# A transformer block on one core: four engines taken off their fixed slot and given one written-out order for all eight batches

## The reference

```python
# branch 1: one-head attention and a layer norm
att = softmax((xn Wq)(xn Wk)^T / sqrt(128))
y   = einsum('bqk,bvd->bqd', att, v)        # k and v summed apart: row sums of att times the sum of v
h   = xn + y Wfc^T + b_fc
o1  = layernorm(h) * gamma + beta
# branch 2: causal attention with 16 heads of 8, then four experts
hn  = rms(xn) * n1_w
q, k, v = rms(heads(hn wq)) * qn_w, rms(heads(hn wk)) * kn_w, heads(hn wv)
ao  = softmax(where(causal, q k^T / sqrt(8), -inf)) v wo^T ; ao[:, :, :32] = 0
x1  = xn + ao ; xf = rms(x1) * n2_w
wts = top 2 of softmax(xf gate^T), scaled to sum 1
moe = sum_e wts[e] * expert_e(xf)           # gelu, silu and two chains of gelu layers
moe[:, :, :32] = 0
out = x + o1 + x1 + moe
```

## Time and profile before

| what | value |
|---|---|
| median of 3 runs | 232.24 us (230.71, 232.24 and 232.61) |
| span of the profiled execution, first to last instruction | 231.3 us |
| PE busy | 202.3 us, 87% of the span |
| DVE busy | 160.1 us, 69% |
| ACT busy | 160.1 us, 69% |
| POOL busy | 112.9 us, 49% |
| mean granted TensorE clock | 0.991 |

### The profile page before, as it was taken

The page is one execution under the profiler, slowest core; times in us unless marked ns, Lnnn a source line. Parts: engine busy times, 40 slices in busy tenths (PEclk is TensorE's granted clock), DMA queues, the critical chain, the costliest instruction groups (busy, mean ns, idle before and its releaser), DMA issues.

```text
span 231.3 us, 6236 instructions
## 1 busy us (share of the span) xinstructions
PE 202.3 (87%) x2132; PEld 145.6 (63%) x2132; DVE 160.1 (69%) x608; ACT 160.1 (69%) x310; POOL 112.9 (49%) x227
## 2 busy tenths in 40 slices
PE   0542898859999999999999999999999999997883
PEld 0311455436867787678767776867686777766563
DVE  2245059795858897789868995899489667847704
ACT  2123447745989698978898789878987998732730
POOL 3834225872572747282837282737375437506000
PEclk9999999997999999999999999999999999999999
DMA  4900100000000020002000200020000000100000
GB/s 124 389 16 11 37 3 1 4 0 0 4 0 3 3 68 6 0 3 68 0 3 6 68 4 0 3 68 4 0 3 27 23 4 0 48 0 3 23 0 27
DMA packets 7570, 6.09 MB, mean 26 GB/s; under 512 B 624, under 2 KB 7024, under 8 KB 7536
## 3 DMA queue, kind: packets, MB, share of 16 engines
q1 hardware_dynamic: 7248, 5.44, 7.5%
q10 hardware_dynamic: 288, 0.21, 0.3%
HBM read 4.60 MB, written 1.05 MB: 24 GB/s over the span
## 4 chain that ended last, share of the span: by engine, by line
PE 73%; DVE 11%; issue 5%; ACT 4%; POOL 3%; DMA 2%; SPq 0%; POOLq 0%; ACTq 0%; DVEq 0%
PE even_ps L1357 12%; PE scores_ps L1242 10%; PE pv_ps L1271 7%; PE odd_ps L1343 7%; PE a_ps L1212 6%; PE even_ps L1343 5%; PE even_ps L1387 4%; PE odd_ps L1387 3%; PE odd_ps L1369 3%; PE a_ps L1184 3%; PE pv_ps L1275 3%; PE a_ps L1286 3%; DMA first<-in_first 2%; DVE acc L1054 2%; PE a_ps L1202 2%
## 5 line engine op out<-in xcount | busy, mean ns | idle before, releaser
L325 POOL TENSOR_SCALAR_AFFINE_SELECT probs<-probs 128x512 f32<-128x512 f32 x64 | 40.3, 635 | 47.4 <-ACT probs L507 46.7
L507 ACT ACTIVATE probs<-scores_ps 128x768 f32<-128x768 f32 x64 | 49.9, 809 | 5.1 <-PE scores_ps L1242 4.9
L1242 PE MATMUL scores_ps<-qT,kT 32*128 32x128 f32 (+1 forms) x512 | 31.4, 361 | 0.3 <-ACT probs L507 0.2
L1357 PE MATMUL even_ps<-l_h,mid 128*128 128x256 f32 x128 | 30.7, 383 | 1.0 <-ACT l_h L569 1.0
L1242 PEld LDWEIGHTS scores_ps<-qT,kT 32*128 32x128 f32 x512 | 24.2, 192 | 10.4 <-issue 9.1
L1357 PEld LDWEIGHTS even_ps<-l_h,mid 128*128 128x128 f32 x128 | 23.4, 190 | 6.2 <-ACT l_h L569 2.1
L1343 PE MATMUL odd_ps<-xfT,up 128*128 128x256 f32 x80 | 22.1, 391 | 0.4 <-DVE acc L1054 0.4
L1271 PE MATMUL pv_ps<-probs,v_aug 128*32 128x256 f32 x256 | 21.3, 406 | 0.9 <-DVE pv_rows L834 0.4
L569 ACT ACTIVATE l_h<-even_ps 128x512 f32<-128x512 f32 x24 | 14.5, 606 | 8.1 <-PE even_ps L1357 7.1
L1212 PE MATMUL a_ps<-qkvT,xnT 128*128 128x384 f32 x32 | 17.5, 635 | 2.1 <-ACT qkv L543 1.5
L1343 PE MATMUL even_ps<-xfT,up 128*128 128x256 f32 x64 | 18.8, 418 | 0.0
(11 more groups left out here) (150 smaller groups left out, 451.4 us busy)
## 6 DMA issues: line engine op xcount, KB each, us to landing
x_sb<-in_x SPq DMA_DIRECT2D x8, 128.0 KB, 2.5
acc<-in_x SPq DMA_DIRECT2D x8, 128.0 KB, 2.1
out<-acc SPq DMA_DIRECT2D x8, 128.0 KB, 1.9
mid<-in_mid SPq DMA_DIRECT2D x1, 640.0 KB, 7.5
up<-in_up SPq DMA_DIRECT2D x1, 578.0 KB, 6.4
downs<-in_down SPq DMA_DIRECT2D x1, 512.0 KB, 8.3
first<-in_first SPq DMA_DIRECT2D x1, 320.0 KB, 5.5
row<-in_rows ACTq DMA_DIRECT2D x1, 200.0 KB, 5.2
```

What stands on the lines that cost most here:

```text
L325: nc.gpsimd.affine_select(out=own, in_=own, compare_op=ALU.is_ge, fill=0.0, base=0, pattern=[[0, 2 * TILES], [1, P]], channel_multiplier=- ...
L507: nc.scalar.activation(probs[g % 2][:, 2 * half:2 * half + 2, 0:SEQ + P], scores_ps[:, 2 * half:2 * half + 2, 0:SEQ + P], ACT.Exp).then_in ...
L1242: ins = T.matmul(ps, kT[p][rows, g, kt * P:(kt + 1) * P], qT[p][rows, kt * P:SEQ], start=kt == 0, stop=kt == 1 and not searching, tile_pos ...
L1357: ins = T.matmul(ps_of(fill)[:, m * SEQ:(m + 1) * SEQ], wT[:, at_col:at_col + P], src[:, ci, :], start=(ci == 0), stop=(ci == HC - 1))
```

## The change

All four engines lose `slot` and get one list of steps for the eight batches, written out call by call (`batches()` on PE and DVE, plain lines on POOL and ACT). The lists have no period: which stage of which batch stands beside which differs from batch to batch. With it:

- The bank of a fill is fixed by name, and its turn is counted as PE's list is issued (`claim`). Bank a holds QKV0, QKV1, QKT, PV0 and PV1, bank b eight narrow fills, even and odd as before.
- `weigh_v` writes two groups into one bank, and `pv_turn` turns 512 columns at once, twice a batch and not four times. `exp_group` takes 1536 columns in one ACTIVATE, `mask` one group in one instruction.
- `probs` has four copies, x_sb, xn and acc eight (so x is loaded once, not twice, and all loads are issued at the start), xnT four, qkv, v_aug, qT, kT, q0T and xfT three, most others two.
- The head normalisation has one cubic and one Newton round, seven steps after the guess, and no halving step. The gate loses two steps (the inverse of the sum and its product) and does four comparisons in two instructions. `fc_row` broadcasts the row sum as its stationary operand, so `a0_xsum` is gone. `scores` of a group waits for that group's copy of k alone.
- In the head DVE clears v_aug (three copies) and computes the flag from a small DMA of its own; PE and DVE read the flag before their first step of `batches()`, and the branch without a search comes first. POOL builds all constants before its first norm step.

```diff
-BANK_FILLS = {
-    "a": (("QKV1", 1), ("Q0T", 1), ("S00", 2), ("S01", 2), ("FC", 2), ("QKT", 1), ("XT", 0), ("QKV0", 0)),
-    "pv": (("PV0", 2), ("XFT", 3), ("GATE", 3), ("PV1", 2), ("PV2", 2), ("PV3", 2), ("WO", 2)),
...
+BANK_OF = {
+    "QKV0": "a", "QKV1": "a", "QKT": "a", "PV0": "a", "PV1": "a",
+    "XT": "b", "Q0T": "b", "S00": "b", "S01": "b", "FC": "b", "XFT": "b", "GATE": "b", "WO": "b",
...
             def weigh_v(n, g):
...
+                pair, half = divmod(g, 2)
+                fill = f"PV{pair}"
+                ps = (claim(fill, n) if half == 0 else ps_of(fill))[:, half * SEQ:(half + 1) * SEQ]
+                pe.wait_ge(s["masked"], GROUPS * n + g + 1)
...
-                ins.then_inc(full_sem(fill), 1)
+                if half == 1:
+                    ins.then_inc(full_sem(fill), 1)
...
+            def batches():
+                x_turn(0); qkv_project(0, 0); fold_weights(); q0_project(0); qkv_project(0, 1); a0_scores(0, 0)
+                a0_scores(0, 1); x_turn(1); qk_turn(0); q0_project(1); find_maxima(0); scores(0, 0); x_turn(2)
...
-            def exp_unit(n, u):
...
+            def mask(n, g):
+
+                pool.wait_ge(s["exp_done"], GROUPS * n + g + 1)
...
+            constants()
+            search_constants(); ln_variance(0); ln_pow(0); h_square(0); h_mean(0); h_eps(0); x1_start(0); h_pow(0)
...
+            def exp_group(n, g):
+                act.wait_ge(s["scores_full"], GROUPS * n + g + 1)
+                if n >= 1:
+                    act.wait_ge(full_sem(f"PV{g // 2}"), at[f"PV{g // 2}", n - 1] + 1)
+                nc.scalar.activation(probs[g][:, :, 0:SEQ + P], scores_ps[:, :, 0:SEQ + P], ACT.Exp
+                                     ).then_inc(s["exp_done"], 1)
...
+            def clear_heads(p):
+
+                V.memset(v_aug[p][:], 0.0).then_inc(s["dve_setup"], 1)
...
+            def pv_turn(n, pair):
```

1945 lines of the change are left out of this document (896 added, 1049 removed), and 4 rows, old and new, of tables (BANK_FILLS, BANK_OF).

## The result

The change takes 233.63 us (median of 20 executions) against 232.69 for the kernel before: ratio 1.0068, 95% interval 1.004 to 1.0096. It is 0.7% **slower**; 228.0 was forecast. The profiled execution has a span of 231.5 us, 0.2 above the 231.3 of before.

The account below looks back on a forecast made before the run. It took PE's work, some 190 us, as the bound, with gains only at the two ends: 231.3 - 5.1 (head) + 2.5 (middle) - 1.6 (tail) = 227.1 of span, plus 0.9 to the median, 228.0 us; range 219 to 236.

Parts of the forecast that it names:

- the middle: Between head and tail: ten more ACT table loads, mostly hidden, cost PE 2.5 us of waits; DVE and POOL at nothing.
- the tail: Batch 7's last layers: held-back down pairs of batch 6 fill gaps, one wait of about 2 stays; 1.6 us won.
- the head: Start to xf(0): 2.1 us sooner, plus 3.0 of PE work done ahead, gives 5.1 us.
- The start: Constants and first norm: first transpose near 7.35, 1.0 us sooner; DVE's branch taken as 0, up to 4.1 possible.
- The loop of scores: Batch 0's scores and exponentials: first scores at 23.9, rounds about 3.5, last scores 34.5, last values 38.0, 2.1 us sooner.
- The chain from there to xf ... unchanged: From batch 0's last values to xf(0): same steps, still 10.9 us, so xf(0) is turned at 48.9.
- the bank of E1A: In the tail, a kernel bank, not a run: L2 of batch 7 waits about 2 us until DVE frees it.
- From span to median: At the sum: 0.9 us added to the span of 227.1, giving a time of 228.0.
- second rival: Head's gain given back: batch 1's chain to xf stays 10.9, PE waits 4 us; span 231, time 232; chance 0.21.
- first rival: ACT's table loads end on PE's path: 239 us, deciding from 9.1 us of PE waits in the middle; chance 0.17.
- 250: Time in us if each extra table load also cost the skill page's drain; chance 0.01.

Follow-up runs that it names:

- e2: The changed kernel with tanh in place of gelu in all experts, so 37 of its 38 table loads go; ratio to the kernel before 0.998, span 230.2 us.
- e3: The kernel before the change with tanh in place of gelu, so 27 of its 28 table loads go; ratio 0.993.
- e9: The changed kernel with DVE's steps for batch 7's heads moved ahead of nine steps of batch 6's gate; 231.11 us, ratio to the kernel before 0.994.
- e13: e9 with 9 unread matmuls added in PE's pauses at 13.7 to 18.9 us; 229.70 us, ratio to the kernel before 0.988.
- e15: e13 with 8 more unread matmuls (4, 1 and 3) in PE's pauses between 30 and 38.7 us; 229.20 us, ratio to the kernel before 0.989.

## Why the prediction was wrong

The span was to be 227.1 and is 231.5. Of these 4.4 us the middle has 2.3 (4.8 lost for 2.5), the tail 1.7 (0.1 lost for 1.6 won) and what follows the last matmul 0.6; the head won 0.6 more than forecast, and 0.4 is the rest of the account above. So the steps that failed are the tail, taken for a gain without a look at DVE's list, and the middle, where all but the loads stood at nothing. Point by point:

- **The start** held: xn(0) turned at 7.55 (7.35 forecast), and the branch on DVE showed nothing, as taken. (The 4.0 us of constants are right, 1.51 to 5.47, though only one of the two clearings that it takes off lies within its 6.63 to 11.81.)
- **The loop of scores** was faster than put: first scores 21.46 (23.9), last 30.04 (34.5), values 35.78 (38.0). Its terms for the first scores add to 22.9 and not to 23.9; with that the head's 5.1 would be 6.1 and the time 227.0, farther from the result. A round took 2.9, not 3.5. And rows of before at half rate stood in view: 1.67 us at 23.21 and 0.94 at 36.64 are the same instructions. The prediction read the second and did not ask what the first was.
- **"The chain from there to xf ... unchanged" failed**: 14.5 us, not 10.9. The steps are the same, but not their neighbours: batch 1's root, and h0 of two batches, stand among them, and 0.7 us of half rate ahead of the output projection. By the rows, 2.3 of the 3.5 lie ahead of that projection (35.78 to 41.80, before 40.06 to 43.74); which neighbour makes them stays open. With that the head gives 0.8 + 3.0 = 3.8 by the prediction's own sum, and 5.7 with the dip of before at 52 to 56, which the prediction also left out. The size 5.1 is about right by luck: its errors cancel.
- **The middle** was mis-sized: 4.8 us of new idle time, not 2.5. The loads' net price (2.2 by e2 and e3) is about what was forecast. The rest is steps on DVE and ACT that PE waits for, which "I cost this at nothing" left out: with the loads gone, e2 still has 2.7 us of waits for DVE and 0.7 for the exponential. That the order or the merges make these waits is read from the trace; no run removes them.
- **The tail failed** in sign: -1.6 forecast, +0.1 measured, and +0.6 behind the last matmul. The wait that it foresaw (about 2, for the bank of E1A) is there, with 1.1; the pause of 2.16 ahead of batch 7's output projection was in no term. The prediction looked at PE's list and not at DVE's, where batch 6's gate stands ahead of batch 7's heads. e9 shows that this alone is 2.1 us in the profile and 2.5 in the median.
- **The rate of PE** was in no term. The change has a mean clock of 0.969, before 0.991; e13 and e15 show 1.2 to 1.9 us.
- **From span to median** it added 0.9, the distance of before's median from the span of one slower execution. Every execution has 1.7 to 1.9 between its span and its time, so a span of 227.1 would be 228.9; the change's median lies 2.1 above its profiled span, by the longer executions.

The result is that of the second rival, no change because the head's gain is given back. Its mechanism, that batch 1's own chain is as long as it was (10.9), holds for the change by the rows, 10.4 us, and fits the three orders of the head (xf(0) sooner, xf(1) not). Its place was wrong: PE idles only 0.6 us between xf(0) and xf(1), and the gain goes in the middle, the tail and the dips, not in one wait of 4 us. The first rival is out: PE's new idle time in the middle stays below the 9.1 us from which it decides.

In the change the first gelu starts 0.02 us behind the end of its load,

```profile
53.82 1.28 ACT L778 ACT_TABLE_LOAD   x1
55.12 0.60 ACT L778 ACTIVATE l_h<-even_ps 128x512 f32<-128x512 f32 x1
```

and the load starts at the end of the exponential ahead of it (52.36 + 1.45). The Trainium skill, ScalarE: Activation LUTs, "What ACT_TABLE_LOAD costs", adds a drain of about 1380 ns to each switch; the trace does not agree. (By that price the prediction's own sum is 252, an estimate, and not 250.)
